# LoRA matrix product by seven block products instead of eight, in an fp32 gated linear layer

## The reference

```python
s = einsum('bsk,nk->bsn', xn, weight * block_mask) + bias          # 32 x 32 blocks on or off
base   = einsum('bsi,oi->bso', xn, W_org)
coeffs = softmax(keys @ (Wq @ mean of xn over the batch) / sqrt(128))    # 8 numbers for each batch
h      = einsum('bsi,eir->bser', xn, lora_down)                     # 8 experts of rank 64
delta  = einsum('be,bser,ero->bso', coeffs, h, lora_up)
out = x + s * silu(base + delta)
```

## Time and profile before

| | |
|---|---|
| median of 3 runs | 437.91 us (437.9 to 438.54) |
| the profiled execution | span 438.5 us from first to last instruction |
| PE busy | 424.7 us, 97% |
| DVE busy | 334.7 us, 76% |
| ACT busy | 216.4 us, 49% |
| POOL busy | 104.9 us, 24% |
| DMA | 101.05 MB, mean 230 GB/s |

### The profile page before, as it was taken

How to read it: one execution, slowest core, us unless ns; L and a number is a source line. 1 busy time by engine, 2 the same in 40 slices (tenths; PEclk the granted TensorE clock), 3 DMA queues, 4 the chain that set the end, 5 groups by cost and what they waited for, 6 DMA issues and landing times.

```text
span 438.5 us, 5903 instructions
## 1 busy us (share of the span) xinstructions
PE 424.7 (97%) x1910; PEld 345.7 (79%) x1910; DVE 334.7 (76%) x492; ACT 216.4 (49%) x379; POOL 104.9 (24%) x91
## 2 busy tenths in 40 slices
PE   6899999999999999999999999999999999999995
PEld 6457888888888878878888788888877887888885
DVE  3898979989989777536578897676757798788735
ACT  2862568996745434414247464254313465445322
POOL 4346040705302122000123001074211220321412
PEclk9899999999999999999999999999999999999999
DMA  8996578866667878899524138879994320287842
GB/s 299 413 416 240 161 266 255 280 210 218 195 237 264 265 290 283 290 325 362 179 73 144 49 114 275 287 236 336 410 386 165 96 76 21 72 270 242 265 160 96
DMA packets 40862, 101.05 MB, mean 230 GB/s; under 512 B 4608, under 2 KB 4864, under 8 KB 40064
## 3 DMA queue, kind: packets, MB, share of 16 engines
q1 hardware_dynamic: 40832, 100.69, 66.7%
HBM read 71.31 MB, written 29.36 MB: 230 GB/s over the span
## 4 chain that ended last, share of the span: by engine, by line
PE 75%; DMA 14%; DVE 4%; POOL 2%; SPq 2%; issue 1%; ACT 1%; DVEq 0%; ACTq 0%; POOLq 0%
PE psA L864 24%; PE psA L866 24%; PE psA L865 24%; DMA x_nat_sb<-in_x_nat_dram 4%; DMA d_dram<-d_split 3%; DMA a_raw<-in_up_dram 2%; DMA out_dram<-cst 2%; DMA worg_sb<-in_w_org_dram 2%; DMA b_hi<-d_dram 2%; PE psA L883 1%; DVE nat_stats L1154 1%; DMA temp<-in_down_dram 1%; SPq L796 1%; DVE cst L1323 1%; POOL x_nat_sb L1365 1%
## 5 line engine op out<-in xcount | busy, mean ns | idle before, releaser
L864 PE MATMUL psA<-b_hi,a_hi 128*128 128x512 f32 (+1 forms) x444 | 173.6, 391 | 0.5 <-ACT snaps L1107 0.5
L866 PE MATMUL psA<-b_hi,a_lo 128*128 128x512 f32 (+1 forms) x444 | 172.1, 388 | 0.0
L865 PE MATMUL psA<-b_lo,a_hi 128*128 128x512 f32 (+1 forms) x444 | 172.0, 387 | 0.0
L864 PEld LDWEIGHTS psA<-b_hi,a_hi 128*128 128x128 f32 x444 | 83.4, 188 | 18.4 <-ACT snaps L1107 0.9
L866 PEld LDWEIGHTS psA<-b_hi,a_lo 128*128 128x128 f32 x444 | 83.4, 188 | 17.1
L865 PEld LDWEIGHTS psA<-b_lo,a_hi 128*128 128x128 f32 x444 | 83.4, 188 | 16.6
L1078 ACT ACTIVATE b_hi<-b_raw 128x512 fp32r<-128x512 f32 (+2 forms) x66 | 45.3, 716 | 56.0 <-DVE b_raw L1232 36.5
L1219 DVE TENSOR_TENSOR b_lo<-b_raw,b_hi 128x512 fp32r<-128x512 f32 (+2 forms) x66 | 52.0, 814 | 8.6 <-ACT b_hi L1078 8.3
L1395 POOL TENSOR_TENSOR cst<-cst,xres 128x512 f32<-128x512 f32 x15 | 23.0, 1534 | 98.7 <-DVE cst L1323 98.7
L1107 ACT ACTIVATE snaps<-psA 128x512 f32<-128x512 f32 x39 | 23.2, 595 | 42.8 <-PE psA L866 42.6
L1219 DVE TENSOR_TENSOR a_lo<-s_raw,a_hi 128x512 fp32r<-128x512 f32 x52 | 37.4, 733 | 5.2 <-ACT a_hi L1068 5.2
(11 more groups left out here) (124 smaller groups left out, 506.3 us busy)
## 6 DMA issues: line engine op xcount, KB each, us to landing
xn_dram<-xq SPq DMA_DIRECT2D x16, 512.0 KB, 5.8
s_dram<-cst SPq DMA_DIRECT2D x32, 256.0 KB, 4.9
worg_sb<-in_w_org_dram SPq DMA_DIRECT2D x32, 256.0 KB, 3.8
xq<-xn_dram SPq DMA_DIRECT2D x16, 512.0 KB, 5.5
s_in<-s_dram SPq DMA_DIRECT2D x32, 256.0 KB, 4.2
xres<-in_x_nat_dram SPq DMA_DIRECT2D x32, 256.0 KB, 4.3
out_dram<-cst SPq DMA_DIRECT2D x31, 256.0 KB, 4.2
x_nat_sb<-in_x_nat_dram SPq DMA_DIRECT2D x14, 512.0 KB, 5.0
```

Source lines behind the costliest of these rows:

```text
L864: nc.tensor.matmul(ps, l_hi, r_hi, start=first, stop=False, skip_group_check=True)
L865: nc.tensor.matmul(ps, l_hi, r_lo, start=False, stop=False, skip_group_check=True)
L866: return nc.tensor.matmul(ps, l_lo, r_hi, start=False, stop=over, skip_group_check=True)
```

## The change

E b.c.t becomes E b.c.p: the LoRA matrix itself is computed by 2x2 blocks with Strassen's seven products p for each of 4 row chunks c. A product is 2 pieces k x 3 matmuls = 6 matmuls of the same shape as before; 28 products for each batch, in two pairs of chunks (0, 1 and 2, 3), each pair going through p = 1, 2, 6, 5, 7, 4, 3. For this:

- D's block sums are made once: DL loads 512 KB (4 pieces), DT makes four sums of 128x256 on DVE (2 of the 16 on POOL), D rounds seven blocks at once (128x1792, ACT), VD makes the lo part in place, DS stores hi and lo apart, 896 KB each; the next DL waits until both are stored. `d_dram` grows from 4 to 7 MB, and is read once for each batch (LD, in 4 groups of blocks for each chunk).
- U's block sums are made for each batch: US scales the 8 pieces in place (ACT), UT makes 8 differences (DVE or POOL), U rounds 14 pieces (ACT), VU makes 14 lo parts (DVE). Ring places hold 6 of them, freed places in `b_hi`/`b_lo` the other 8.
- ES copies chain X's bank after products 1, 6 and 7 (ACT, 12 for each batch), EG adds the W_org tile to the copy (DVE or POOL, 12), and EA adds a bank to that (16, as before). Product 3 waits until EA has read chain Y's bank.
- All five strings of ORDER are new. 8 of the S steps, 6 of the QR steps and 3 of the T steps move from DVE to POOL. PE's string changes in the E steps alone; its P, TX, BP and G steps stand in the same order.

```diff
--- before
+++ after
@@ -36,6 +36,15 @@
 OPERAND_B = {1: B11, 2: B21, 3: B22, 4: T4, 5: T1, 6: T2, 7: T3}
 BLOCK_OF = {2: (0, 0), 7: (1, 1), 4: (1, 0), 3: (0, 1)}
 SETS = (0, 8, 12)
+E_CHAIN = {1: "X", 6: "X", 7: "X", 4: "X", 2: "Z", 5: "Y", 3: "Y"}
+E_BLOCK = {1: 0, 2: 1, 7: 2, 4: 3, 5: 4, 6: 5, 3: 6}
+E_GROUP = ((1, 2), (6, 5), (7, 4), (3,))
+E_SNAP = {0: 1, 1: 6, 3: 7}
+E_DONE = {0: 2, 1: 3, 2: 4, 3: 5}
+U_HOME = {1: B11, 5: T1, 6: B21, 4: B22}
+U_RING = {7: 0, 3: 2, 2: 4}
+UP_TILE = {1: 0, 2: 2, 7: 4, 3: 6}
+WORG_ORDER = [(c + i, t) for c in (0, 2) for t in (0, 1, 3, 2) for i in range(2)]
...
+    US0.2.0 U0.7.0 U0.2.0 U0.6.1 QO57 U0.7.1 U0.3.1 U0.4.0 US0.2.1 ES0.0.0 U0.2.1 H55 ES0.1.0 U0.4.1 HB1.0.0 HB1.0.1
...
+    def e_key(st):
+        return ("E", st[1], st[2], E_CHAIN[st[3]])
+
+    acc_use = number(dict.fromkeys([acc_key(st[1]) if st[0] == "P" else e_key(st) if st[0] == "E" else st
+                                    for st in pe_steps if st[0] in ("P", "E") or by_rows(st)]))
...
-    d_dram = nc.dram_tensor("d_dram", [KC, P, 2, H], F32, kind="Internal").ap()
+    d_dram = nc.dram_tensor("d_dram", [4, P, 2, 7 * HALF], F32, kind="Internal").ap()
...
-        d_split, _ = at("d_split", [P, 2, H], F32R, temp_at)
+        d_raw, _ = at("d_raw", [P, 7 * HALF], F32, temp_at)
+        d_lo, _ = at("d_lo", [P, 7 * HALF], F32R, temp_at)
...
+        d_hi, _ = at("d_hi", [P, 7 * HALF], F32R, r1_at)
...
+        def u_free(eng, b, o, k):
+
+            if o in U_HOME:
+                eng.wait_ge(pe_P, index[(SETS[b + 1] - 1, {1: 1, 5: 5, 6: 2, 4: 3}[o])] + 1)
+            else:
+                eng.wait_ge(pe_P, op_last[u_ring(b, o, k) - ARING] + 1)
+
+        def u_home(tiles, ring, b, o, k):
+            if o in U_HOME:
+                return tiles[:, U_HOME[o], 2 + k, :]
+            return ring[:, u_ring(b, o, k) % ARING, :]
+
+        def u_raw(b, o, k):
+            return temp[:, 2 + k, :] if o == 4 else u_home(b_raw, a_raw, b, o, k)
...
+        def d_operand(c, p, half, k):
+
+            blk = E_BLOCK[p]
+            if blk == 6:
+                cols = slice(half * HALF + k * P, half * HALF + (k + 1) * P)
+                return d_snaps[:, 2 * (c % 2), cols]
+            cols = slice(blk % 2 * HALF + k * P, blk % 2 * HALF + (k + 1) * P)
+            return b_hi[:, (T2, T4, T3)[blk // 2], 2 * (c % 2) + half, cols]
+
...
+        def ut_operands(b, j, k):
+            u11, u12, u21, u22 = [u_raw(b, o, k) for o in (1, 7, 2, 3)]
+            return {1: (u_raw(b, 5, k), u12, u11), 2: (u_raw(b, 6, k), u22, u_raw(b, 5, k)),
+                    3: (u12, u22, u12), 4: (u_raw(b, 4, k), u21, u_raw(b, 6, k))}[j]
...
+        def dt_operands(j):
+            a11, a12, a21, a22, s1, s2, s4 = [d_raw[:, i * HALF:(i + 1) * HALF] for i in range(7)]
+            return {1: (s1, a21, a22, ALU.add), 2: (s2, s1, a11, ALU.subtract), 3: (a21, a11, a21, ALU.subtract),
+                    4: (s4, a12, s2, ALU.subtract)}[j]
...
                 elif kind == "DL":
-                    k = st[1]
-                    if k == 0:
+                    c = st[1]
+                    if c == 0:
                         wait_lo(sp, ("B", 0, T1, 0))
                     else:
-                        wait_lo(sp, ("D", k - 1))
-                    sp.dma_start(temp[:, 3, :], down_t[k]).then_inc(d_loaded, 16)
+                        sp.wait_ge(d_stored, 32 * c)
+                    sp.dma_start(d_raw[:, 0:4 * HALF].rearrange("p (a n) -> p a n", a=2), down_t[c]).then_inc(d_loaded, 16)
                 elif kind == "DS":
-                    k = st[1]
-                    wait_lo(sp, ("D", k))
-                    sp.dma_start(d_dram[k], d_split[:, :, :].bitcast(F32)).then_inc(d_stored, 16)
+                    _, c, lo = st
+                    if lo:
+                        wait_lo(sp, ("D", c))
+                        sp.dma_start(d_dram[c][:, 1, :], d_lo[:, :].bitcast(F32)).then_inc(d_stored, 16)
+                    else:
+                        wait_hi(sp, ("D", c))
+                        sp.dma_start(d_dram[c][:, 0, :], d_hi[:, :].bitcast(F32)).then_inc(d_stored, 16)
                 elif kind == "LD":
-                    _, b, k = st
+                    _, b, c, g = st
                     last = SETS[b + 1] - 1
-                    sp.wait_ge(d_stored, 16 * KC)
-                    if k == 6:
+                    sp.wait_ge(d_stored, 32 * 4)
+                    if c >= 2:
+                        for p in E_GROUP[g]:
+                            wait_product_E(sp, b, c - 2, p)
+                    elif g == 3:
                         for i in (2, 3):
                             wait_block(sp, index[(last - 1, i)])
-                    elif k == 7:
-                        for i in (7, 2):
-                            wait_block(sp, index[(last, i)])
                     else:
-                        sp.wait_ge(pe_P, index[(last, (7, 7, 4, 4, 6, 6)[k])] + 1)
-                    sp.dma_start(d_tile(k).bitcast(F32), d_dram[k]).then_inc(dhl_loaded[k], 16)
+                        sp.wait_ge(pe_P, index[(last, (6, 7, 4)[g])] + 1)
+                    first = (0, 4, 2, 6)[g] * HALF
+                    sp.dma_start(d_group(g, c).bitcast(F32), d_dram[c][:, :, first:first + (HALF if g == 3 else H)])\
+                      .then_inc(dhl_loaded[c % 2][g], 16)
...
                 elif kind == "E":
-                    _, b, c, t = st
-                    bank = take_acc(st)
-                    d = d_tile(c + 4 * (t // 2))
-                    pe.wait_ge(dhl_loaded[c + 4 * (t // 2)], 16 * (b + 1))
-                    for k in range(4):
+                    _, b, c, p = st
+                    first = p in (1, 2, 5)
+                    bank = take_acc(e_key(st)) if first else acc_bank(e_key(st))
+                    if p in (6, 7, 4):
+                        wait_snap_E(pe, b, c, {6: 0, 7: 1, 4: 3}[p])
+                    elif p == 3:
+                        wait_E(pe, b, c, 3)
+                    g = [p in group for group in E_GROUP].index(True)
+                    pe.wait_ge(dhl_loaded[c % 2][g], 16 * (2 * b + c // 2 + 1))
+                    for k in range(2):
                         if c == 0:
-                            wait_lo(pe, ("U", b, 4 * (t % 2) + k))
-                        slot = u_slot(b, 4 * (t % 2) + k)
-                        ins = triple(bank, d[:, 0, k * P:(k + 1) * P], d[:, 1, k * P:(k + 1) * P],
-                                     a_hi[:, slot, :], a_lo[:, slot, :], k == 0, k == 3)
+                            wait_lo(pe, ("U", b, p, k))
+                        ins = triple(bank, d_operand(c, p, 0, k), d_operand(c, p, 1, k), u_home(b_hi, a_hi, b, p, k),
+                                     u_home(b_lo, a_lo, b, p, k), k == 0 and first, k == 1)
                     ins.then_inc(pe_E, 1)
...
+                elif kind == "US":
+                    _, b, o, k = st
+                    act.wait_ge(up_loaded[UP_TILE[o] + k], 16 * (b + 1))
+                    act.wait_ge(dve_coef, b + 1)
+                    row = u_row(o, k)
+                    nc.scalar.activation(u_raw(b, o, k), u_raw(b, o, k), ACT.Copy, scale=coef[:, b, row:row + 1])\
+                        .then_inc(act_scaled, 1)
...
                 elif kind == "D":
-                    k = st[1]
-                    act.wait_ge(d_loaded, 16 * (k + 1))
-                    if k:
-                        act.wait_ge(d_stored, 16 * k)
-                    nc.scalar.activation(d_split[:, 0, :], temp[:, 3, :], ACT.Copy).then_inc(act_hi, 1)
+                    c = st[1]
+                    for j in (3, 4):
+                        wait_DT(act, c, j)
+                    if c:
+                        act.wait_ge(d_stored, 32 * c)
+                    else:
+                        act.wait_ge(act_stat, len(x_num))
+                    nc.scalar.activation(d_hi[:, :], d_raw[:, :], ACT.Copy).then_inc(act_hi, 1)
+                elif kind == "ES":
+                    _, b, c, t = st
+                    wait_product_E(act, b, c, E_SNAP[t])
+                    nc.scalar.activation(e_raw(c, t), acc_bank(("E", b, c, "X")), ACT.Copy).then_inc(act_snap_E, 1)
...
                 elif kind == "EA":
                     _, b, c, t = st
-                    e = e_num[(b, c, t)]
-                    dve.wait_ge(worg_loaded[e % 4], 16 * (e // 4 + 1))
-                    dve.wait_ge(pe_E, e_num[(b, c, t)] + 1)
-                    nc.vector.tensor_tensor(e_raw(c, t), acc_bank(("E", b, c, t)), worg_tile(b, c, t), ALU.add)\
-                        .then_inc(dve_E, 1)
+                    wait_product_E(dve, b, c, E_DONE[t])
+                    bank = acc_bank(("E", b, c, {0: "Z", 1: "Y", 2: "X", 3: "Y"}[t]))
+                    if t == 2:
+                        wait_worg(dve, b, c, t)
+                        nc.vector.tensor_tensor(e_raw(c, t), bank, worg_tile(b, c, t), ALU.add).then_inc(dve_E, 1)
+                    else:
```

(7 more changed lines are left out.)

326 lines of the change are left out of this document (211 added, 115 removed).

## The result

| | before | after |
|---|---|---|
| median of 4 runs, us | 438.23 | 485.2 |
| lowest to highest, us | 437.9 to 439.39 | 484.8 to 486.31 |
| ratio after / before | | 1.1053 (95% interval 1.1001 to 1.1104) |
| profiled execution: span, us | 438.5 | 483.1 |
| its mean granted clock of PE | 0.996 | 0.958 |

The change makes the kernel 10.5% slower. The forecast was 427.7 us.

The account below looks back on a forecast made before the run. PE was taken to bound the kernel: -10.9 (matmuls), -0.5, -0.95, -1.66 (old waits), +1.8 (D), +1.6 (U), +0.4 (W_org) make -10.2 us, so 427.7 from 437.9; own range 425 to 430, 8 in 10 423.5 to 433.5.

Parts of the forecast that it names:

- The price of a matmul, and how many go: E stages on PE: 48 fewer matmuls at 0.228 us each take 10.9 us off.
- PE sets the time: Whole kernel: PE, busy 97% of the span, bounds it; a matmul less saves time if nothing else is late.
- neither becomes the bound: E0: DVE, busy 27.9 of 44.8 us, and ACT, busy 15.8, were said not to become the limit.
- DVE 355 of 428, 83%: Whole span: DVE's busy time forecast after the change, 335 + 20 us.
- The D chain: Before P58: four serial rounds through ACT, DVE and SP, 16.9 us each, delaying PE by 1.8 us.
- The slower rival: D steps hold ACT and, through snapshots of P42 and P49, PE; slower than before from 21.3 us a round; chance 0.08.
- The term of 1.8 us: Ahead of E0: PE's delay from D's rounds at 16.9 us each.
- 3p - 51.9: Ahead of E0: PE's delay through P49's snapshot, p being the length of one D round in us.
- PE's other steps keep their order: Outside the E products: PE's order stays, so the 10.9 us saved is nearly the whole effect on PE.
- 37 more POOL steps at 0.37: DVE beside POOL: each added POOL step hinders DVE by 0.37 us, 14 us in all, within DVE's slack.
- 48 us at worst: DVE beside POOL: 37 steps at 1.3 us if they exclude one another wholly, DVE at 94% and late in E stages.
- 0.8 us for each batch: Start of each E stage: U's last piece between 0 and 2.4 us late, taken as 0.8, 1.6 in all.

Follow-up runs that it names:

- b_triple_r: The kernel before with each of its 16 row sums on VectorE done three times; 464.8 us, ratio 1.0543.
- b_moved: The kernel before with its S, T and QR steps on the engines the changed kernel puts them on; 440.98 us, ratio 1.0012.
- a_both: The changed kernel with all 37 added GpSimd steps on VectorE instead; 474.79 us, ratio 1.0771.
- b_column: The kernel before, eight products kept, in the changed kernel's order by column blocks, with the steps reading the results moved accordingly; 463.76 us, ratio 1.0545.

## Why the prediction was wrong

**The price of a matmul, and how many go: right.** 48 fewer, and 0.228 us apart wherever PE doesn't wait.

**"PE sets the time": true, and too little.** The step from the page's shares to "neither becomes the bound" failed. "DVE 355 of 428, 83%" is a mean over stretches; from P24 to P44 DVE had 5.0 us to spare, and the change puts DT, longer VD and hindered steps there. b_triple_r shows the rule without the change: 38 us of work at 80% of the span costs 24.

**The D chain: mechanism right, term wrong.** The slower rival said that a D step ahead of P42's and P49's snapshots holds them up from p = 21.3. The round came out at 21.1 and PE waited 4.3 us for P42's snapshot, and lost 1.4 more at half pace behind it; for P49's it didn't wait. But I built the round from transfers with 2.7 us for the sums. The transfers were no longer than forecast, 9.2 us at the medians for a load and a lo store where 10.0 were; the 4 us by which the round was longer are DVE's queue: 6.3 us from the end of D to the start of VD in the first round, 4.8 for the four sums of the third. The term of 1.8 us measured 5.6 by that wait and what followed it; by its own formula, 3p - 51.9, a round of 21.1 makes 11.4.

**The rest of the stretch ahead of E0: put at nothing.** It came out 13.5 us longer. The snapshot of P33 wasn't in the working at all: PE waited 4.0 us for it and lost 1.5 behind it. By the strings and the trace that is because DVE now does VD0 and S steps ahead of QC31; no kernel tests it. "PE's other steps keep their order" held for PE, and said nothing of what stands ahead of their snapshots on ACT and DVE. No DT gives 8.6 back; of the other single edits none gave more than 5.2 there. The loads of the split D landed sooner than before (KB each, median us to landing; 8.1 before), answering to the earlier trace rows:

```profile
b_hi<-d_dram SPq DMA_DIRECT2D x24, 512.0 KB, 6.7
```

**DVE and POOL: I chose the wrong end.** "37 more POOL steps at 0.37" came from one overlap. Timelines of POOL (two rows) and DVE (two) in the changed kernel, answering to the earlier trace rows:

```profile
341.53 2.81 POOL L1571 TENSOR_TENSOR a_raw<-a_raw 128x512 f32<-128x512 f32 x1 [11.37 <-ACT a_raw L1233]
344.30 1.29 POOL L1587 TENSOR_TENSOR cst<-cst,xres 128x512 f32<-128x512 f32 x1
...
342.49 0.69 DVE L1385 TENSOR_TENSOR a_lo<-a_raw,a_hi 128x512 fp32r<-128x512 f32 x1
344.47 1.66 DVE L1385 TENSOR_TENSOR b_lo<-b_raw,b_hi 128x512 fp32r<-128x512 f32 x1 [1.29 <-POOL a_raw L1571]
```

The POOL step at 341.53 ends 1.2 us after DVE's last step beside it (343.18), as if it began then; DVE's at 344.47 ends 0.5 after POOL's (345.59), so it ran almost wholly behind it. I summed what DVE's two-operand steps after 60 us took over an unhindered one of their width: 11.1 us before, 24.6 in b_moved, 57.5 after, 25.9 in a_both. For each step on POOL more that is 0.8 (17 steps, b_moved), 0.85 (37, after against a_both) and 1.25 (37, after against before). The rule of the Trainium skill, "SBUF — State Buffer", on its two separate sides, that the two exclude one another for the whole instruction, agrees with these rows. The prediction's 48 us at worst by that rule compares with 46 measured (57.5 less 11.1). In the kernel's time it is 12 us.

**U: size wrong.** 0.8 us for each batch; PE waited 4.25 and 5.06 for U2. (The upper end of 2.4 was added wrongly as well: 2.6 + 0.7, and 3.5 - 1.4 = 2.1 for what follows the product, are 5.4 and not 5.8, so 2.0 late.) The late load is one part (the DMA share of 192 to 214 us in a_both is 1.0), the place of U2 behind other pieces the other: moved ahead, 2.5 of 2.8 us went in E0, 0.5 of 3.9 in E1.

**Inside E, and behind it: a step missing.** "PE's other steps keep their order" was said of PE, and nothing was said of the order in which the new products finish the operands of the next ones. That is the largest omission: +5.0 and +7.8 us in the two stretches of a_both, +7.8 and +10.1 in b_column, where 5.5 are waits for V steps that I had put late. It belonged to the change itself: results by column pair in place of by quadrant stand in the rows of PE's order.

**The clock: not priced.** Each microsecond of waiting was counted as one. The seven waits of 3.3 us and more were each followed by 6 to 13 slow matmuls, at a cost of 1.4 to 2.75 us each, 13.1 of the 15.1 us of slower pace. In six cases they began at once; behind the wait of 3.39 us that ended at 389.73 they began 1.3 us later. The granted clock (the third number from the end) was 0.50 there, the lower of the two levels, 1.2 GHz:

```profile
211.50:217.00 5.50, 5.50 (x13) 4.34 (x14) 4.81 (x9) 1.20 (x2) 0.00 (x0) 0.50 0.42 132
391.30:394.60 3.30, 3.20 (x8) 2.48 (x8) 2.94 (x6) 1.42 (x4) 2.02 (x2) 0.50 0.00 0
```

The parts, against before: exclusion 12 us (2.8%); sums of D on a full DVE 10 (1.0771 - 1.0532); W_org's additions 7; the place of U2 and T 4; the order of the results 10 (a_both's P59 to P64 and P87 to P92) to 18 (b_column, with its V steps). They come to 43 to 51 us. To be explained are 58, the 47 by which the kernel is slower and the 10.9 that the matmuls gave. The 7 to 15 us between are not settled by an experiment. Most of it lies ahead of E0, where a_both is 16.7 over the kernel before and the sums of D gave back 8.6; the waits for the snapshots of P33 and P53 stand there in the traces, but no kernel moves what holds them. No kernel takes transfers away either, and from 192 to 214 us a_both's DMA engines are at a share of 1.0. The parts also overlap (W_org's additions stand in the stretches by which the order is measured), so none of them is exact to better than some 3 us.

## What to carry to other kernels

Read the slack of an engine by stretches, against the steps of the engine that sets the time, before adding work to it: 5 us in 56 was the figure that mattered, not 24% of the span. Trading 11 us of TensorE for some 40 of vector work (VectorE is busy for 53 us more in a_both, 15 of them hindrance) pays only where the vector work falls into idle time and the trade leaves results coming in the order in which they are used. Where a step stands on one engine decides which snapshot is late on another: follow each step that is put in to the next step that frees a bank. Here a step moved to GpSimd to relieve VectorE took more of VectorE than it gave, when both worked on two SBUF operands.

## What the runs showed of the hardware

- A GpSimd sum of two SBUF operands cost VectorE 0.8 to 1.25 us of hindrance, against 0.69 for doing it there: DVE's busy time fell by 9 us when it got 37 steps more.
- Each of the 36 waits of 3.3 us and more after start-up, in twelve of the fourteen kernels (`before` and `b_moved` have none), was followed by 6 to 14 matmuls about 0.43 us apart in place of 0.228, at a cost of 1.4 to 3.0 us. They began up to 1.3 us after the wait's end. Of the 28 waits of 2.0 to 3.2 us 15 were followed so and 13 were not, so the length of the wait alone doesn't decide it.
